# Genes product split over two column halves, with a third pass in the product behind it

## What is computed

```python
logits = jnp.einsum('btd,gd->btg', xn, Wc) / jnp.clip(temperature, 0.1)
top_vals, top_idx = jax.lax.top_k(logits, N_ACTIVE)      # 32 of 1024
expr_w = jax.nn.softmax(top_vals, axis=-1)
expressed = jnp.einsum('btk,btkc->btc', expr_w, genes[top_idx])   # 64 numbers a token
down = jnp.tanh(jnp.einsum('btc,dc->btd', expressed, Wd))
up = jnp.einsum('btc,dc->btd', expressed, Wu)
return down * xn * up * scale
```

## Time and profile before

| | us |
|---|---|
| median of the runs | 510.07 |
| profiled execution, its own time | 507.2 |
| its span, first to last instruction | 505.4 |
| TensorE matmuls busy | 432.6 (86%) |
| VectorE busy | 386.5 (76%) |
| ScalarE busy | 273.5 (54%) |
| GpSimd busy | 257.3 (51%) |
| mean granted clock of TensorE | 0.953 of full |

### The profile page before, as it was taken

The page is one execution under the profiler, slowest core; times in us unless marked ns, Lnnn a source line. Parts: engine busy times, 40 slices in busy tenths (PEclk is TensorE's granted clock), DMA queues, the critical chain, the costliest instruction groups (busy, mean ns, idle before and its releaser), DMA issues. The chain is left out here.

```text
span 505.4 us, 11005 instructions
## 1 busy us (share of the span) xinstructions
PE 432.6 (86%) x3866; PEld 341.5 (68%) x3866; DVE 386.5 (76%) x611; ACT 273.5 (54%) x418; POOL 257.3 (51%) x263
## 2 busy tenths in 40 slices
PE   0645778989999999999999999999999998885824
PEld 0534456768888888787777777777778776673613
DVE  4584143698989898989888888888989888868470
ACT  3661626474757575757575757565757563542211
POOL 1363535556666666666666665657474753031121
PEclk9987689999999999999999999999999998998857
DMA  7931324140414141414141404141323222000000
GB/s 246 325 69 28 76 64 87 32 93 25 96 44 95 45 95 46 93 43 93 43 94 32 101 27 100 35 93 42 82 53 75 61 56 51 2 22 0 21 21 21
DMA packets 82027, 34.45 MB, mean 68 GB/s; under 512 B 73152, under 2 KB 75216, under 8 KB 82000
## 3 DMA queue, kind: packets, MB, share of 16 engines
q1 hardware_dynamic: 81040, 33.05, 27.8%
q10 hardware_dynamic: 960, 1.05, 0.7%
HBM read 12.86 MB, written 4.19 MB: 34 GB/s over the span
## 5 line engine op out<-in xcount | busy, mean ns | idle before, releaser
L400 POOL TENSOR_TENSOR stage_b<-stage_b,cos_t 128x512 f32<-128x512 f32 x32 | 40.9, 1279 | 111.3 <-issue 60.1
L855 DVE TENSOR_REDUCE row_max<-psum 128x8 f32<-128x1024 f32 x64 | 75.4, 1220 | 19.7 <-PE psum L1150 19.3
L917 DVE MAX8 top<-stage_b 128x8 f32<-128x1024 f32 x64 | 78.5, 1226 | 12.1 <-ACT stage_b L636 9.7
L926 DVE MATCH_REPLACE8 stage_b<-top,stage_b 128x1024 f32<-128x1024 f32 x64 | 77.5, 1211 | 0.6 <-issue 0.3
L446 POOL TENSOR_TENSOR down<-down,kept 128x512 f32<-128x512 f32 x16 | 20.6, 1290 | 105.7 <-ACT down L665 105.7
L636 ACT ACTIVATE stage_b<-psum,rstd 128x512 f32<-128x512 f32 x32 | 22.0, 688 | 83.7 <-PE psum L1073 83.7
L600 ACT ACTIVATE stage_a<-psum 128x1024 f32<-128x1024 f32 x64 | 63.5, 1022 | 0.0
L1073 PE MATMUL psum<-wcT_h,yT_h 128*128 128x512 f32 x128 | 54.2, 424 | 4.0 <-DVE yT_l L903 3.2
L1073 PE MATMUL psum<-wcT_l,yT_h 128*128 128x512 f32 x128 | 51.5, 402 | 0.0
L1073 PE MATMUL psum<-wcT_h,yT_l 128*128 128x512 f32 x128 | 51.1, 399 | 0.0
L1194 PE MATMUL psum<-stage_a,v_ext 128*32 128x128 f32 x1024 | 38.0, 284 | 3.6 <-ACT stage_a L600 3.0
(11 more groups left out here) (128 smaller groups left out, 1038.8 us busy)
## 6 DMA issues: line engine op xcount, KB each, us to landing
x_ring<-x_dram SPq DMA_DIRECT2D x16, 256.0 KB, 2.6
out_dram<-x_ring SPq DMA_DIRECT2D x16, 256.0 KB, 2.0
ctx_sb<-ctx_dram SPq DMA_DIRECT2D x16, 128.0 KB, 2.6
stage_a<-L_ffn_Wc_dram SPq DMA_DIRECT2D x1, 2048.0 KB, 11.1
stage_b<-L_xattn_Wq_dram ACTq DMA_DIRECT2D x1, 1024.0 KB, 5.7
stage_b<-L_xattn_Wkv_dram SPq DMA_DIRECT2D x2, 512.0 KB, 9.0
stage_b<-L_xattn_Wout_dram SPq DMA_DIRECT2D x1, 1024.0 KB, 13.5
genes_sb<-L_ffn_genes_dram SPq DMA_DIRECT2D x2, 256.0 KB, 5.2
```

The lines of the kernel that those rows point to most:

```text
L400: pool.tensor_tensor(halves(qk_cos), halves(qk_sb), trig(cos_t, t), ALU.mult).then_inc(s_cosm[n], 1)
L855: nc.vector.tensor_reduce(row_max[:, 0:HEADS].rearrange("p (odd m) -> p odd m", odd=2)[:, :, 4 * g:4 * g + 4], score_of[g][:].rearrange("p ...
L917: nc.vector.max(top[:, 8 * n:8 * n + 8], logit if n == 0 else rest).then_inc(s_top[n], 1)
L926: nc.vector.match_replace(rest, top[:, 8 * n:8 * n + 8], logit if n == 0 else rest, REMOVED).then_inc(s_rem[n], 1)
```

## The change

genes_sb holds the genes once. express sends even chunks to partitions 0 to 63 of the PSUM bank and odd chunks to 64 to 127, each as a matmul with 64 columns of weights; the two sums are not added. Both copies of the transposed weights are awaited first. e_hi and e_lo write two tensors of 128 rows, eT_h and eT_l. As the weights stand twice along the rows, the product over 128 rows adds even and odd chunks, and down_up takes three passes.

```diff
-        genes_sb = sb("genes_sb", [P, GK, 2 * GD])
+        genes_sb = sb("genes_sb", [P, GK, GD])
...
-        eT_hl = sb("eT_hl", [2 * GD, P], f32r)
+        eT_h, eT_l = sb("eT_h", [2 * GD, P], f32r), sb("eT_l", [2 * GD, P], f32r)
...
-            for half in range(2):
-                sp.dma_start(genes_sb[:, :, half * GD:(half + 1) * GD],
-                             genes.rearrange("(g p) c -> p g c", p=P)).then_inc(s_genes, 16)
+            sp.dma_start(genes_sb[:], genes.rearrange("(g p) c -> p g c", p=P)).then_inc(s_genes, 16)
...
-                nc.scalar.activation(eT_hl[:], bank("eT")[:, 0:P], ACT.Copy).then_inc(s_eT_h, 1)
+                nc.scalar.activation(eT_h[:], bank("eT")[:, 0:P], ACT.Copy).then_inc(s_eT_h, 1)
...
-                nc.vector.tensor_tensor(eT_hl[GD:2 * GD], bank("eT")[GD:2 * GD, 0:P],
-                                        eT_hl[GD:2 * GD].bitcast(f32), ALU.subtract).then_inc(s_eT_l, 1)
+                nc.vector.tensor_tensor(eT_l[:], bank("eT")[:, 0:P], eT_h[:].bitcast(f32),
+                                        ALU.subtract).then_inc(s_eT_l, 1)
...
-                    pe.wait_ge(s_genes, 32)
-                for n in (1, 0):
+                    pe.wait_ge(s_genes, 16)
+                for n in range(2):
                     pe.wait_ge(s_wTr[n], t + 1)
-                    for g in range(4 * n, 4 * n + 4):
-                        last = nc.tensor.matmul(bank("eT")[:, 0:P], genes_sb[:, g], gene_wT[:, g * P:(g + 1) * P],
-                                                start=(g == 4), stop=(g == 3))
+                for g in range(GK):
+                    rows = slice(GD * (g % 2), GD * (g % 2) + GD)
+                    last = nc.tensor.matmul(bank("eT")[rows, 0:P], genes_sb[:, g], gene_wT[:, g * P:(g + 1) * P],
+                                            start=(g < 2), stop=(g >= GK - 2))
                 last.then_inc(s_eT, 1)
...
-                nc.tensor.matmul(gene_out[n], eT_hl[:], wduT_h[:, cols], start=True, stop=False)
-                nc.tensor.matmul(gene_out[n], eT_hl[:], wduT_l[:, cols], start=False,
-                                 stop=True).then_inc((s_dn, s_upp)[n], 1)
+                nc.tensor.matmul(gene_out[n], eT_h[:], wduT_h[:, cols], start=True, stop=False)
+                nc.tensor.matmul(gene_out[n], eT_h[:], wduT_l[:, cols], start=False, stop=False)
+                nc.tensor.matmul(gene_out[n], eT_l[:], wduT_h[:, cols], start=False, stop=True).then_inc((s_dn, s_upp)[n], 1)
```

## The result

The changed kernel takes 517.91 us (median of 4 runs, 516.13 to 518.47), the kernel before on the same chip 509.87 (509.35 to 510.09). The ratio is 1.0153 with an interval of 1.0127 to 1.0179: 1.5% slower, where 1.1% was forecast; 2.0 us above the forecast value and inside the range of 513.6 to 518.8. It is 0.3 us above 517.6, where the forecast's own spread ended; the rest of the range had been added for rival 3. The profiled execution of the changed kernel took 516.13 us (its span 514.3), against 507.2 and 505.4 before, so the span grew by 8.9 us.

What follows compares the result with a forecast made beforehand. The prediction took a ring of TensorE (project_out to logits(0)) and VectorE (cT_l to aT_l) as the bound. Its terms summed to +5.8 us, 507.2 to 513.0 profiled, 515.9 median; own spread 513.6 to 517.6, range 513.6 to 518.8.

Steps and rivals of the forecast that it cites:

- rival 3: In express, the halves do not pair, so it costs 0.13 more instead of 0.75 less: 519.1 us, chance 0.10.
- The ring: Loop pass: TensorE from project_out to logits(0), then VectorE from cT_l to aT_l; the third pass adds 0.47 us.
- Express: Gene product on TensorE, outside the ring: eight pairs save 0.75 us, which in the loop becomes longer waiting for aT_l.
- the values rows: Profile rows of the values product (L1194), used to price express: each further set of four records costs 0.11 us.
- cT_l's wait up by nearly 0.5: VectorE in the loop: cT_l's wait for ScalarE, 1.26 us before, was to grow by nearly 0.5.
- +0.09 and +0.37: Added time of the two passes after the first with an express before it, from project_out starts 130.35 and 155.59.
- The pass of the last tile of x and the next: After the loop: +0.47 up to the k projection; then one down_up hidden, and express saves 0.43 of its 0.75.
- The granted clock in the tail: Tail: down_up at 482.98 at the lower clock, +0.87; last down_up possibly there too, +1.2, 517.1, within the spread.
- The last tile's later start: Last tile: express waits for both copies and starts 0.75 us later; 0.35 net saving taken.
- Rival 1: TensorE is the bound throughout and the saving counts everywhere: 4.2 us less, 505.9 us, chance 0.03.
- Rival 2: The third passes of down_up are partly hidden, so 4.8 of the 5.8 us vanish: 510 us, chance 0.04.
- rival 4: Longer idle lets the granted clock fall in the loop: above 525 us, chance 0.03; last down_up low: 517.1.

Runs made afterwards that it cites:

- e1: Kernel before, full-width express, with the low-weight matmul of down_up issued twice (six matmuls instead of four): 517.11 us, ratio 1.0149.
- e2: Changed kernel with the half-width express but without the third pass of down_up: 509.61 us, ratio 1.0014.
- e5: Changed kernel with two VectorE moves, aT_l ahead of find_top 1 and e_lo ahead of x_lo: 504.16 us, ratio 0.9879.
- e6: Kernel before with two VectorE moves, aT_l ahead of find_top 1 and e_lo ahead of x_lo: 506.62 us, ratio 0.9938.
- e8: The changed kernel run once more, unchanged: 518.58 us, ratio 1.018.
- e7: e5 with express taking each half of the chunks as its copy of the weights arrives, instead of awaiting both: 503.11 us, ratio 0.9882.
- e3: Changed kernel with aT_l moved ahead of find_top 1 on VectorE: 509.3 us, ratio 0.9981.
- e4: Kernel before with aT_l moved ahead of find_top 1 on VectorE: 506.33 us, ratio 0.9939.

## Why the prediction was right, and where it was not

- **The ring, and express outside of it: right.** Passes of the loop cost 0.42 us more (0.47 forecast), by e1 all of it from the third pass, and the wait for aT_l grew by 0.65 to 0.82 (0.7 forecast). e2 and e5 against e6 show it from both sides: nothing from the halves with the ring closed, 0.25 a pass with it open.
- **Express: right, a little small.** 0.86 us saved in the timeline for 0.75; with TensorE as the bound, 0.72 net. The estimate from the values rows, pairs at 0.11, held to the record. Eight pairs at 0.11 are 0.88, so 0.15 of the 1.03 us are left for the first weights and both switches of shape together; the prediction had 0.26. Of the 0.14 between 0.86 and 0.72, 0.05 stands behind the transposes of x, from which project_out starts after 0.41 us at the earliest in e5 and after 0.36 in e6; the rest isn't located. The Trainium skill (TensorEngine Tiling (Array Packing), Key Properties) has a change of tiling mode drain the engine; these 0.15 us leave room for that, and no run here separates the drain from the weight loads.
- **The sign of "cT_l's wait up by nearly 0.5": wrong.** It stayed at 1.26. The prediction put VectorE's added idle time at the last point before the ring's own half; it shows at three points before that (0.19, 0.27 and 0.38 above), because x_ring and row_max each follow TensorE too, and combine does by way of tanh and the gate. The sum doesn't rest on it.
- **The two passes before the loop: +1.75 for +0.46.** The terms +0.09 and +0.37 counted matmuls alone. In the first of the two the scores wait for a stretched transposing DMA, which the prediction had at nothing (see the last section). The last matmul of project_q and the scores start 1.11 us apart instead of 0.32, and this 0.79 is the whole excess of the pass (26.1 us, where 25.33 was forecast). The second takes 26.10 for 25.62, of which later scores show 0.11; the other 0.37 stays open.
- **The pass of the last tile of x and the next: right, but for the clock.** The table's -0.27 and -1.15 for +0.47 and -0.43 come in part from where it cuts. The prediction counts up to the scores behind the transposing DMA, the table up to project_out. TensorE's rows at the scores and at the fourth matmul of the first logits half, after and then before (the scores of before are in the earlier trace rows):

```profile
424.33 0.40 PE L1148 MATMUL psum<-kT,qT 64*128 64x128 f16 x8 [2.39 <-DMA kT<-parts]
...
427.91 0.40 PE L1071 MATMUL psum<-wcT_h,yT_h 128*128 128x512 f32 x1
```

```profile
424.32 0.40 PE L1073 MATMUL psum<-wcT_h,yT_h 128*128 128x512 f32 x1
```

  From project_out at 386.95 to the scores at 419.27 are 32.32 us before, from 391.54 to 424.33 32.79 after: +0.47, as forecast. The express between them lets project_out start 0.27 earlier, and the wait for the DMA takes that back (2.39 for 2.13). From the scores to the next project_out are 17.09 us before and 15.20 after, -1.89 for -0.43. Of this, 1.47 is gained up to the fourth logits matmul (5.05 and 3.58 us), where the kernel before has the lower clock and the changed one has not. The remaining -0.42 is the forecast's -0.43.
- **The granted clock in the tail: named, too small.** Before, the lower level stands in 26.7 us after 400 us, after in 39.4. Three pieces of it show in the table. The kernel before is at the lower level from 420.7 to 424.1 and the changed one is not, which is the 1.47 above. The changed one is at it from 447.6 to 454.4, under the twelve matmuls of the first logits half, and the one before is not. The windows of both stretches, before and then after (the clock is the third number from the right):

```profile
420.00:425.00 5.00, 5.00 (x65) 3.89 (x64) 4.35 (x5) 1.19 (x2) 2.84 (x4) 0.66 0.16 57
447.00:455.00 8.00, 7.95 (x51) 6.73 (x50) 4.19 (x8) 2.83 (x5) 0.47 (x1) 1.00 0.01 2
```

```profile
420.00:425.00 5.00, 2.61 (x20) 1.83 (x19) 4.34 (x8) 3.25 (x4) 2.67 (x3) 1.00 0.82 155
447.00:455.00 8.00, 7.21 (x50) 5.52 (x51) 2.84 (x4) 1.74 (x4) 4.03 (x4) 0.57 0.09 35
```

  The last down_up stands at the lower level after and not before. TensorE's rows, after and then before:

```profile
449.17 0.76 PE L1071 MATMUL psum<-wcT_h,yT_h 128*128 128x512 f32 x1 [0.79 <-ACT stage_b L604]
449.74 0.63 PE L1071 MATMUL psum<-wcT_l,yT_h 128*128 128x512 f32 x1
450.16 0.63 PE L1071 MATMUL psum<-wcT_h,yT_l 128*128 128x512 f32 x1
...
504.64 0.79 PE L1277 MATMUL psum<-wduT_h,eT_h 128*128 128x512 f32 x1 [0.69 <-DVE eT_l L946]
505.23 0.63 PE L1278 MATMUL psum<-wduT_l,eT_h 128*128 128x512 f32 x1
...
506.94 0.63 PE L1279 MATMUL psum<-wduT_h,eT_l 128*128 128x512 f32 x1
```

```profile
497.43 0.50 PE L1278 MATMUL psum<-wduT_h,eT_hl 128*128 128x512 f32 x1 [0.69 <-DVE eT_hl L948]
...
498.23 0.40 PE L1279 MATMUL psum<-wduT_l,eT_hl 128*128 128x512 f32 x1
```

  Starts 0.42 us apart instead of 0.235 make the twelve matmuls 2.4 us longer (5.26 us from 449.17, for 2.90); with the 0.46 that the forecast has for the third pass that is 2.8 of the +3.11. From the first to the last start of the last down_up are 2.30 us for 0.80: +1.50, where +0.47 was forecast as the central value and another 1.2 for this case as part of the spread. Whether the clock stands low at 447 us follows from what happens to fall together there and isn't the change alone: in the second profile of the same kernel the first low stretch is at 427.7 to 431.1 instead, the other three lie within 0.7 us of where they were, 36.0 us in all, and the tail is 1.2 us shorter. With that stretch just behind the scores of the same pass as in the kernel before, the three passes behind the loop come out as forecast (+0.46 for +0.50, by e8).
- **The last tile's later start: right** (0.80 for 0.75, by e7), and most of the shorter express there was spent on it: from the transposes of gene_w to down_up are 5.37 us after and 5.61 before, 0.24 saved where 0.35 was forecast.
- **Rivals.** Rival 3 (no pairs) is out by the records. Rival 1 is out in the loop. In the pass of the last tile of x alone project_out does start earlier, by 0.27, and the wait for the DMA takes it back. Rival 2 asked for 4.8 us to vanish; the eight passes alone kept 3.35 of their 3.76. Of rival 4 the loop's part is out (granted clock 1.00), the last down_up's came true.

Set against the forecast, the errors are -0.13, +1.29, -0.41, -0.74, -0.72, +2.65 and +1.20 by the rows of the table: 5.1 us upward and 2.0 downward, 3.1 us in the profiled span. In the medians it is 2.0, because the forecast puts the median 2.9 us above the profiled execution, as it was before, and it came out 1.8 above. The large errors are mostly of the clock and the DMA, not of the ring. That the two signs cancel in part, and that the profiled execution lay nearer to its median, is luck. So is part of the range: the clock of the last down_up, named as 517.1, came true, and the measured 517.91 is still above the own spread of 517.6 and inside only by the part kept for rival 3, which the records put out.

## What to carry to other kernels

Before pricing an edit, find which half of the ring each of its parts lies in: work added to the ring counts in full, work taken from beside it turns into a longer wait. If the wait that swallows a saving ends on an engine with a queue of independent steps, look first at the order of that queue, since the same edit can be worth +0.42 or -0.25 us a pass by the place of two steps in it. After opening one wait, read the list of waits again before judging: e3 had only changed which value was late.

## What the runs showed of the hardware

**A transposing DMA with a 16 KB packet of the instruction queue inside takes longer.** In the pass from 129.84 the DMA view shows one 16 KB packet of the instruction queue among the transposes of q and k, and both issues take longer to land. The stretch from 131 to 138 us, after and then before (queue, kind: packets, MB, share; issue, count, us from issue to landing):

```profile
q8 instruction: 1, 0.02, 0.8%
...
qT<-parts SPq DMA_TRANSPOSE x1, 6.2
kT<-parts SPq DMA_TRANSPOSE x1, 6.8
```

```profile
qT<-parts SPq DMA_TRANSPOSE x1, 4.4
kT<-parts SPq DMA_TRANSPOSE x1, 5.6
```

The scores wait for it, 0.79 us longer than before; in the pass after it, with such a packet too, 0.11 us:

```profile
139.21 0.40 PE L1148 MATMUL psum<-kT,qT 64*128 64x128 f16 x8 [0.72 <-issue]
```

From the first to the last packet of a tile's two transposes the trace of after has 6.16 and 6.26 us in these two passes and 5.08 to 5.16 in thirteen of the other fourteen. Over ten traces with 160 such pairs, all 13 with a 16 KB packet of that queue inside took 6.02 to 6.27 us, and the 147 others 5.07 to 5.74. The packets come only in the passes outside the loop (none between about 215 and 415 us). e1 and e4 each have one such pass at 26.11 and 26.06 us, the kernel before has none, the repeated after kernel three. (e4 and e6 also have a pass of 26.06 and 26.08 without one, so the length of a pass alone is no sign of it.) The third one of the repeat is in the pass before these two: 25.21 us with the packet, 24.38 in the first profile without it. So in the first of the two passes here 0.79 us go with where a packet happened to fall. The same kernel has two in one profile and three in the other. What sets the moment stays open, and since no run tried to shift it alone, that the packet is the cause is argued from these counts.

**The last down_up and the clock.** In all six profiles with the half-width express (after, its repeat, e2, e3, e5, e7) the last down_up stands at the lower level of 1.2 GHz, in all four with the full width (before, e1, e4, e6) at the upper. In after, TensorE ends express at 503.94 and the level stays low to the end; before, express goes on to 496.73 and the level rises at 495.8 under it. Behind the shorter product its successor is slower: 0.43 us a matmul for 0.235. No experiment held the width and changed only the length of express, so that its length is the cause is argued, not shown.
